# A recommender tower: one-hots move to GpSimd, selected fields change slots, loads and orders change

## The reference

```python
e = jnp.stack([tbl_0[ids[:, 0]], ..., tbl_49[ids[:, 49]]], axis=1)   # 512 x 50 x 16
gram = jnp.einsum('bid,bjd->bij', e, e)
z = gram[:, I, J]                                    # i < j, 1225 values
h = jnp.concatenate([z, dense_ctx], axis=1)
h = jnp.maximum(h @ W_top1 + b_top1, 0.0)            # 1241 -> 512
h = jnp.maximum(h @ W_top2 + b_top2, 0.0)            # 512 -> 256
y = h @ W_top3                                       # 256 -> 1
```

## Time and profile before

| | us |
|---|---|
| median of three runs (lowest, highest) | 158.98 (158.74, 159.48) |
| the profiled execution, its own time | 159.45 |
| its span, first to last instruction | 157.3 |
| PE busy | 127.8 (81%) |
| POOL busy | 124.7 (79%) |
| DVE busy | 110.6 (70%) |
| ACT busy | 44.4 (28%) |
| mean granted clock of PE | 0.975 |

### The profile page before, as it was taken

How to read it: one execution, slowest core, us unless ns; L and a number is a source line. 1 busy time by engine, 2 the same in 40 slices (tenths; PEclk the granted TensorE clock), 3 DMA queues, 4 the chain that set the end, 5 groups by cost and what they waited for, 6 DMA issues and landing times.

```text
span 157.3 us, 3325 instructions
## 1 busy us (share of the span) xinstructions
PE 127.8 (81%) x1323; PEld 111.9 (71%) x1323; DVE 110.6 (70%) x193; ACT 44.4 (28%) x77; POOL 124.7 (79%) x184
## 2 busy tenths in 40 slices
PE   0007875937698999999999989999995994999992
PEld 0007764827588679978959989886695983899991
DVE  1807899998899989998898894999953019344021
ACT  8930000232205220332071205204422018444020
POOL 2989898898998989899889889898988898982000
PEclk9999998696899999999999999999999999999998
DMA  3199999734380010000000100010000000000000
GB/s 84 35 358 419 442 417 317 279 116 119 125 256 15 6 6 4 10 7 4 10 6 4 10 4 6 11 10 6 4 10 6 4 10 4 10 6 6 0 0 1
DMA packets 6486, 12.40 MB, mean 79 GB/s; under 512 B 2077, under 2 KB 5414, under 8 KB 6342
## 3 DMA queue, kind: packets, MB, share of 16 engines
q1 hardware_dynamic: 3592, 11.46, 19.7%
q0 software_dynamic: 2880, 0.74, 5.6%
HBM read 12.17 MB, written 0.03 MB: 78 GB/s over the span
## 4 chain that ended last, share of the span: by engine, by line
POOL 70%; PE 14%; issue 9%; DMA 3%; ACT 2%; DVE 1%; DVEq 0%
POOL moving L294 50%; POOL spacer L300 20%; PE psm L818 4%; PE gram L811 4%; DMA moving<-tbl,ids_sb 2%; PE gram L818 2%; PE p L818 2%; DMA ids_sb<-in_ids 1%; PE gram L792 1%; PE pt L878 1%; ACT blocks L214 1%; DVE mcols L542 1%; ACT scols L344 0%; PE pt L868 0%; DVE h2w L604 0%
## 5 line engine op out<-in xcount | busy, mean ns | idle before, releaser
L294 POOL DMA_INDIRECT moving<-tbl,ids_sb x90 | 89.3, 992 | 17.4 <-issue 14.6
L777 PE MATMUL psm<-table,onehot 128*128 128x160 f32 x208 | 36.7, 326 | 19.3 <-DVE onehot L510 12.8
L777 PEld LDWEIGHTS psm<-table,onehot 128*128 128x128 f32 x208 | 32.2, 206 | 22.3 <-issue 12.8
L818 PE MATMUL p<-z,w_sb 128*128 128x128 f32 x312 | 39.3, 276 | 2.3 <-DVE z L225 2.3
L818 PEld LDWEIGHTS p<-z,w_sb 128*128 128x128 f32 x312 | 37.1, 192 | 3.6 <-ACT z L225 1.8
L300 POOL MEMSET spacer<- 128x288 f32 x90 | 35.4, 394 | 0.0
L498 DVE TENSOR_TENSOR picked<-psm,mask 128x480 f32<-128x480 f32 (+1 forms) x36 | 22.1, 634 | 4.5 <-PE psm L777 4.2
L214 ACT COPY blocks<-mcols 32x384 f32<-32x384 f32 (+3 forms) x20 | 15.4, 771 | 32.4 <-DVE mcols L542 21.2
L220 DVE COPY z<-gram 63x384 f32<-63x384 f32 (+1 forms) x20 | 9.6, 480 | 17.3 <-PE gram L811 14.0
L482 DVE TENSOR_REDUCE fixed<-picked 128x48 f32<-128x480 f32 (+1 forms) x36 | 21.3, 627 | 0.2
L767 PE MATMUL psm<-large_table,large_hot 125*128 125x400 f32 x48 | 16.9, 501 | 0.0
(11 more groups left out here) (50 smaller groups left out, 86.5 us busy)
## 6 DMA issues: line engine op xcount, KB each, us to landing
wide<-quotients SPq DMA_DIRECT2D x4, 896.0 KB, 8.2
w_sb<-in_w SPq DMA_DIRECT2D x1, 3072.0 KB, 17.4
large_table<-tbl SPq DMA_DIRECT2D x2, 781.2 KB
moving<-tbl,ids_sb POOLq DMA_INDIRECT x90, 2.8
table<-in_small SPq DMA_DIRECT2D x1, 720.0 KB, 7.2
table<-in_small SPq DMA_DIRECT2D x1, 640.0 KB, 8.7
w_sb<-in_w SPq DMA_DIRECT2D x1, 512.0 KB
table<-in_small SPq DMA_DIRECT2D x1, 480.0 KB, 5.9
```

Of the source, the lines that this page charges most:

```text
L294: nc.gpsimd.indirect_dma_start(moving[:, t, slot, 0:D], None, table, bass.IndirectOffsetOnAxis(ap=ids_sb[:, t, field:field + 1], axis=0),) ...
L777: ins = nc.tensor.matmul(psm[:, m % 2, (f - a) * R * D:(f - a + 1) * R * D], onehot[:, t % 2, f, :], table[:, f, :], start=True, stop=True)
L818: return nc.tensor.matmul(hidden_sums(t, k), w1_sb[:, c, P * k:P * (k + 1)], z[:, t % 2, c, :], start=first, stop=last)
```

## The change

- `SELECTED` becomes [1, 2, 2, 2]: one picked field of tile 0 is selected too (unit 9), so there are 89 gathers. The picked fields come first among the large ones and take the first two middle slots; `fold` writes there, and `turn_mid` waits for them, `turn_late` no longer.
- After gathers 13 to 21, 23 to 35 and 41 to 53, GpSimd makes one-hots of two small fields each (`pool_onehots`, 35 of them: fields 9 to 25 of tile 1, all of tiles 2 and 3) and no memset. VectorE no longer makes these; it was eight instructions of 8 or 9 fields.
- The two large tables are loaded ahead of w1. ids_t and consts are issued by ScalarE.
- The product of zeros goes: the first chunk starts the sum itself. So does the memset of `quot_t`. `large_masks` covers four tiles and has buffers of its own.
- The orders on ScalarE, VectorE and PE are written anew. On PE, product_y(0) now comes after ten selections of tile 0 and three of tile 1 (nine and five before).

The core of the diff:

```diff
-SELECTED = [0, 2, 2, 2]
+SELECTED = [1, 2, 2, 2]
-LARGE[len(LARGE) // 2 + 1:len(LARGE) // 2 + 1] = PICKED
+LARGE[0:0] = PICKED
+HOT_FIELDS = 2
+HOT_BEGINS = {1: 12, 2: 22, 3: 40}
+FIRST_HOT = {0: 26, 1: 9, 2: 0, 3: 0}
+VECTOR_HOTS = [3, 4, 4, 4]
...
         def _(sp):
             sp.dma_start(ids_sb[:], ids).then_inc(ids_loaded, 16)
-            sp.dma_start(ids_t_sb, ids_t).then_inc(ids_t_loaded, 16)
-            sp.dma_start(consts[:], consts_in).then_inc(consts_loaded, 16)
...
                 if t >= 2:
-                    sp.wait_ge(wide_ready, NWC * (t - 1))
+                    sp.wait_ge(wide_ready, VECTOR_HOTS[t - 2])
+                    if t > 2:
+                        sp.wait_ge(pool_ready, pool_hots(t - 2, NS))
                     sp.wait_ge(large_ready, sum(SELECTED[:t - 1]))
...
             load_wide(1)
+            for n in range(NP):
+                sp.dma_start(large_table[0:UNITS, n], tables[n].rearrange("(q p r) d -> p q (r d)", q=SPLIT, r=RL)
+                             ).then_inc(large_loaded, 16)
             sp.dma_start(w1_sb[:], w1.rearrange("p (c n) -> p c n", c=CH)).then_inc(w1_loaded, 16)
...
             load_wide(2)
-            for n in range(NP):
-                sp.dma_start(large_table[0:UNITS, n], tables[HALF + n].rearrange("(q p r) d -> p q (r d)", q=SPLIT, r=RL)
-                             ).then_inc(large_loaded, 16)
             load_wide(3)
...
+                count[0] += 1
+                for tile, began in HOT_BEGINS.items():
+                    first = FIRST_HOT[tile] + HOT_FIELDS * (count[0] - 1 - began)
+                    if FIRST_HOT[tile] <= first < NS:
+                        pool_onehots(tile, first, min(first + HOT_FIELDS, NS))
+                        return
+                clear_spacer()
+
+            def pool_onehots(t, a, b):
+
+                if a == FIRST_HOT[t]:
+                    pool.wait_ge(wide_loaded[t], 16)
+                    if t == 1:
+                        pool.wait_ge(consts_loaded, 16)
+                    else:
+                        pool.wait_ge(rows_made, unit(t - 2, NSC))
+                nc.gpsimd.tensor_scalar(onehot[:, t % 2, a:b, :],
+                                        wide[:, t % 2, P * a:P * b].rearrange("p (f b) -> p f b", b=P),
+                                        consts[:, 0:1], None, ALU.is_equal).then_inc(pool_ready, 1)
...
         def _(act):
+            act.dma_start(ids_t_sb, ids_t).then_inc(ids_t_loaded, 16)
+            act.dma_start(consts[:], consts_in).then_inc(consts_loaded, 16)
...
-                dve.wait_ge(mid_gathered[t], 16 * HALF)
+                dve.wait_ge(mid_gathered[t], 16 * (HALF - SELECTED[t]))
+                if SELECTED[t]:
+                    dve.wait_ge(folded, unit(t, NSC + SELECTED[t]))
...
-                    if n == 0 and whole == CH:
-                        nc.tensor.matmul(p1[:], quot_t[SIDE:SIDE + 1, 0:P], quot_t[SIDE:SIDE + 1, :],
-                                         start=True, stop=False)
                     for k in range(H1 // P):
-                        ins = chunk_sum(t, c, k, n == 0 and whole < CH, n == CH - 1 and k == H1 // P - 1)
+                        ins = chunk_sum(t, c, k, n == 0 and (k == 0 or whole < CH), n == CH - 1 and k == H1 // P - 1)
```

The new order up to product_y(0) and behind it, on VectorE (left: what stands between the last folds of tile 0 and the first unloading) and on PE:

```diff
             large_masks()
+            turn_smalls(0)
+            pick(0, 9)
+            onehots_large(1, 0)
+            fold(0, 9)
+            onehots_large(1, 1)
+            turn_mid(0)
             pick(1, 0)
+            copy_mid(0)
             pick(1, 1)
-            turn_smalls(0)
-            turn_mid(0)
             pick(1, 2)
-            copy_mid(0)
...
-            selections(0, 0, 9)
-            selections(1, 0, 5)
+            selections(0, 0, 10)
+            selections(1, 0, 3)
             product_y(0)
+            selections(1, 3, 5)
             layer0 = first_layer(0)
+            chunks(layer0, 1)
+            selections(1, 5, 7)
             chunks(layer0, 4)
...
+            chunks(layer0, 1)
+            product_y(1)
             second_layer(0)
-            product_y(1)
...
+            selections(2, 6, 9)
             product_x(1, 0)
+            selections(2, 9, 11)
+            chunks(layer1, 2)
...
+            chunks(layer1, 2)
+            selections(3, 4, 6)
+            product_y(2)
...
+            chunks(layer2, 2)
+            second_layer(1)
             product_x(2, 0)
-            chunks(layer2, 7)
+            chunks(layer2, 8)
             second_layer(2)
             product_y(3)
             second_bias(3)
+            layer3 = first_layer(3)
+            chunks(layer3, 2)
             product_x(3, 0)
-            layer3 = first_layer(3)
             chunks(layer3, 4)
             product_x(3, 1)
-            chunks(layer3, 5)
+            chunks(layer3, 4)
             product_x(3, 2)
-            chunks(layer3, 2)
+            chunks(layer3, 1)
             second_layer(3)
```

More of the change, by code:

```diff
@@ L71, with pool_hots @@
 CONSTS = 5 + SPLIT + RL
+HOT_BEGINS = {1: 12, 2: 22, 3: 40}
+FIRST_HOT = {0: 26, 1: 9, 2: 0, 3: 0}
+VECTOR_HOTS = [3, 4, 4, 4]
+def pool_hots(t, b):
+    return sum(-(-(NS - FIRST_HOT[n]) // HOT_FIELDS) for n in range(1, t)) + -(-(b - FIRST_HOT[t]) // HOT_FIELDS) if t else 0
 def unit(t, u):
@@ L492, in pick @@
                     a, b = u - NSC, u - NSC + 1
-                    rows, which = RL, large_mask[:, t - 1, a:b, :]
+                    rows, which = RL, large_mask[:, t, a:b, :]
                 k = b - a
@@ L609, in _ @@
             onehots(0, 2)
+            onehots_large(0, 0)
             pick(0, 0)
@@ L642, in _ @@
             unload_y(0)
-            onehots(1, 2)
-            onehots(2, 0)
-            onehots(2, 1)
-            onehots(2, 2)
             pick(1, 3)
             pick(1, 4)
+            fold(1, 3)
             turn_late(0, 0)
             pick(1, 5)
+            pick(1, 6)
             copy_late(0, 0)
-            fold(1, 3)
             fold(1, 4)
             fold(1, 5)
-            pick(1, 6)
+            fold(1, 6)
             pick(1, 7)
+            pick(1, 8)
+            fold(1, 7)
+            fold(1, 8)
             unload_x(0, 0)
-            pick(1, 8)
             unload_pairs(0)
-            fold(1, 6)
-            fold(1, 7)
-            pick(1, 9)
-            fold(1, 8)
-            fold(1, 9)
+            turn_smalls(1)
             onehots_large(2, 0)
+            smalls(1, 9, 10)
             onehots_large(2, 1)
-            turn_smalls(1)
-            pick(1, 10)
+            smalls(1, 10, 11)
+            turn_mid(1)
+            copy_mid(1)
             pick(2, 0)
-            fold(1, 10)
+            pick(2, 1)
             fold(2, 0)
-            pick(2, 1)
-            turn_mid(1)
+            fold(2, 1)
             pick(2, 2)
-            onehots(3, 0)
-            copy_mid(1)
-            fold(2, 1)
+            pick(2, 3)
             fold(2, 2)
-            onehots(3, 1)
-            onehots(3, 2)
-            pick(2, 3)
-            pick(2, 4)
             fold(2, 3)
             unload_y(1)
-            pick(2, 5)
-            fold(2, 4)
-            fold(2, 5)
+            last_layer(0)
+            smalls(2, 4, 6)
+            turn_late(1, 0)
+            copy_late(1, 0)
             pick(2, 6)
@@ L691, in _ @@
             fold(2, 7)
-            pick(2, 8)
-            last_layer(0)
-            fold(2, 8)
-            turn_late(1, 0)
+            smalls(2, 8, 9)
+            unload_x(1, 0)
+            unload_pairs(1)
+            turn_smalls(2)
             pick(2, 9)
-            copy_late(1, 0)
             pick(2, 10)
-            turn_smalls(2)
-            pick(3, 0)
             fold(2, 9)
             fold(2, 10)
-            unload_x(1, 0)
-            fold(3, 0)
-            unload_pairs(1)
-            pick(3, 1)
-            pick(3, 2)
-            fold(3, 1)
-            fold(3, 2)
             onehots_large(3, 0)
             onehots_large(3, 1)
+            pick(3, 0)
+            pick(3, 1)
+            fold(3, 0)
+            fold(3, 1)
             turn_mid(2)
+            copy_mid(2)
+            pick(3, 2)
             pick(3, 3)
-            copy_mid(2)
+            fold(3, 2)
             fold(3, 3)
@@ L719, in _ @@
             fold(3, 5)
-            last_layer(1)
-            smalls(3, 6, 7)
+            unload_y(2)
+            pick(3, 6)
             pick(3, 7)
-            pick(3, 8)
+            fold(3, 6)
             fold(3, 7)
-            fold(3, 8)
-            unload_y(2)
+            smalls(3, 8, 9)
+            pick(3, 9)
             turn_smalls(3)
             turn_late(2, 0)
-            pick(3, 9)
+            pick(3, 10)
             copy_late(2, 0)
             fold(3, 9)
-            smalls(3, 10, 11)
+            fold(3, 10)
+            last_layer(1)
             unload_x(2, 0)
@@ L988 @@
         "ids": ids.reshape(P, TILES * F),
```

(2 more changed lines are left out.)

104 lines of the change are left out of this document (47 added, 57 removed).

## The result

The changed kernel takes 185.59 us (median of 4 runs, 184.62 to 186.10) against 159.23 for the kernel before: ratio 1.165, 95% interval 1.158 to 1.171. The prediction said 161.0 with a range from 155.3 to 166.5. The direction was the forecast one, the size was far outside. The profiled execution took 185.38, its span is 182.3, 25.0 more than before. Some executions of a kernel take over 1.5% longer than its fastest, and the ratios leave those out.

A forecast was written before the change was run, and what follows sets the result against it. Gathers decide when the tail starts, PE its length. POOL: -1.47 - 2.5 + 3.2 + 5.0 = +4.2, less 2.2 slack, +2.0; PE +1.5; the later counts: span 159.3, median 161.0, range 155.3 to 166.5.

The forecast's parts named there:

- (c): On POOL, 35 one-hots of 256 elements replace memsets, at 0.45 us each: +3.2 us (bounds -0.9 and +6.9).
- 1.8 cycles an element: Second estimate for a POOL one-hot of 256 elements: 0.48 us in all, making the POOL sum 1 us higher.
- 2.2 us of slack: Between the last gather's columns being ready (145.48) and product_x(3,2) starting (147.66); taken off POOL's +4.2, leaving +2.0.
- the one-hots on POOL cost much: Rival, chance 0.12: at 0.55 us a one-hot the last gather moves 3.5 us more, median 164.5; at 0.65, 168.
- (d): On POOL, tile 2's first one-hot waits for wide(2) behind gather 23, from 39.3 to 45.1: +5.0 us (bounds 1 and 6).
- (b): Eight one-hots leave VectorE, so POOL's gathers and memsets are held up less: -2.5 us (bounds -4 and 0).
- (a): On POOL, one gather less: -1.47 us for the last gather.
- The large tables ahead of w1: Tables land at 32.3, so pick(0,9) starts at 35.1, not 31.0, and product_y(0) at 41.1, 4.6 us later.
- the half clock: PE's four 400-column products before pick(0,9) take 5.5 us at half clock; 2.8 was taken, 5.5 kept for the range.
- in time: Rival, chance 0.36: tables land by 28.2, product_y(0) starts at 37.0, PE ends 2.6 us earlier; span 154.7, median 156.4.
- PE after product_y(0): PE's stretch: 117.7 less 6.4 idling, plus 0.7 work and 2.6 remaining idling; last product at 155.7, +1.5 us.
- One-hots of GpSimd held up by VectorE's large ones: VectorE's two-input large one-hots may block POOL's one-hots, which read: at most 7 x 0.69 = 4.8 us.

The follow-up runs named there:

- form runs: Kernel before with its 90 memsets replaced by ten forms of instruction on scratch tiles, nine in a row each; TENSOR_SCALAR of 256 took 0.877 to 0.956 us, copies 0.40.
- d_dummy: Kernel before with 35 of its 90 memsets replaced by one-hots of a scratch tile that nobody reads; 191.44 us against 159.31, once.
- a_vector: Changed kernel with all one-hots back on VectorE and a memset behind every gather, large tables still early; 168.81 us against 159.31, ratio 1.064.
- h3_split: Changed kernel with one-hots back on VectorE and each large table loaded in two parts, 112 and 13 partitions; 158.95 us, ratio 1.004 (kernel before 158.62).
- h2_split: Same kernel as h3_split, run on a chip where the kernel before takes 184.94; 195.36 us, ratio 1.055.

## Why the prediction was wrong

*The step that failed* is (c) of POOL, the term "I take 0.45, between them since nothing is nearer to one: +0.09 x 35 = +3.2 (bounds -0.9 and +6.9)". It measured +24.9 (0.72 x 34 + 0.40). The price was drawn from the memset's rate, once for a write, twice for a read and a write. The form runs show that this is right for a copy (0.40, between 0.33 and 0.55) and wrong for TENSOR_SCALAR, which takes 2.6 ns an element. The upper bound of +6.9 was none: nothing in the trace of before said that the rate of one instruction of GpSimd holds for another. The estimate by the Trainium skill's 1.8 cycles an element ("GPSIMD Engine Reference", section 3.1) was too low for this instruction as well, 0.48 against 0.95; measured, 2.6 ns an element is some 3 cycles of the 1.2 GHz that the page gives, and the fixed part is three times the 0.10 that I put beside it. Section 4.1 of the same page of the Trainium skill has it that one-input work "is roughly line-rate"; the copies come nearer to that (0.40 us for 256 elements), this instruction doesn't.

*The mechanism around it was right in the main*: the gather queue decides when the tail starts, and a longer instruction there moves every later gather. d_dummy shows it with nothing else of the change. *The path was not*: the sum led from the last gather, less 2.2 us of slack, to product_x(3,2). The end hung at the last middle gather instead, where the kernel before has no slack either (product_y(3) waits 2.02 for it). By the prediction's path 25.4 less 2.2 would be 23.2 us; the measured 25.0 are 21.6 at product_y(3) and 3.4 in the tail. The rival "the one-hots on POOL cost much" had the mechanism, too, with 0.12 and a price of 0.55 to 0.65.

*(d), the stall at wide(2)*: forecast 5.0, measured 3.9; it began at 45.3, since the one-hots of tile 1 had already moved gather 23 by 6.6, and it ended at 49.2, not 45.1. So that the length came out near is partly luck. *(b), fewer hold-ups*: forecast -2.5, found -1.9 as the rest of a sum. *(a)* needs no measurement: it is one repeat of the queue less.

*The large tables ahead of w1*: forecast landing 32.3, measured 36.9; the half clock, which I put into the range only, came true, after PE had stood 12.7 us. 4.6 + 2.5 = 7.1 explain the 6.8 us by which product_y(0) was later than forecast. The rival "in time" falls. That the few engines are the cause, the split loads show. Why the landing was 4.6 later than the rate from the earlier trace rows isn't settled; w1 flowed beside the tables from 24 us on, which my sum left out.

*PE after product_y(0)*: the sum 117.7 - 6.4 + 0.7 + 2.6 = 114.6 was hidden in the change, but a_vector and h3_split lay it open: 114.8 us from product_y(0) to PE's last product in the first (47.54 to 162.29), 114.5 in the second (38.40 to 152.89). The total is so close partly by luck: PE idles 4.3 and 3.5 us, not 2.6, and is busy 110.5 and 111.0, not 112.0. Against the kernel before, h3_split gains 5.0 us from product_y(0) to product_y(3) (91.1 in place of 96.2) and loses 1.9 ahead of it and 1.7 in the tail; that is the 1.5 between the spans 155.8 and 157.3. The median of h3_split's ten runs, 158.95, is above what its profiled execution (157.57) gives: such a difference is beyond what a sum over one execution can tell.

*One-hots of GpSimd held up by VectorE's large ones*, by the Trainium skill's "SBUF — State Buffer", section on who interferes with whom: at most 4.8 us was put beside the sum. The trace of the changed kernel has two places where such instructions overlap, by 0.3 us each, and neither side takes longer than elsewhere. The first:

```profile
67.12 0.96 POOL L332 TENSOR_SCALAR onehot<-wide,consts 128x256 f32<-128x256 bf16 x1
67.75 0.69 DVE L559 TENSOR_TENSOR large_hot<-wide,consts 128x512 f32<-128x512 bf16 x1 [0.35 <-PE psm L796]
```

All 34 one-hots together take 0.6 us more than 34 x 0.95, so whatever held them up, it wasn't 4.8. Two short overlaps are too few to speak against the rule.

## What to carry to other kernels

An instruction that takes the place of another on the engine whose queue paces the kernel is priced by itself, in its own form, on the chip, before anything is arranged around it: ten forms fit in one run. A rate taken from another instruction of the same engine bounds nothing from above. A load that few DMA engines carry (125 partitions: 5.2 of 16 here) belongs behind everything that is urgent, or is cut so that most of it goes over more of them (112 + 13 for 125 brought it 10 us forward). And the slack of a queue is read at the first place where the limiting engine waits for it, here product_y(3), not at its last instruction.

## What the runs showed of the hardware that was not expected

TENSOR_SCALAR on GpSimd costs over twice a copy of the same size (0.95 and 0.40 us for 256 elements), in all types and both operations tried, and the gather behind it takes 1.03 us in place of 0.95.

Gathers that follow each other without a memset between them (every 1.25 us) leave VectorE waiting up to 14.5 us at a time for what the profile calls remote, and PE up to 15.4 us; the last such wait of VectorE ends at 126.8, 10 us after the last gather. The memsets may be there for that. It was one run, on a chip where the kernel before takes 200.7, and the cause wasn't isolated.

The same kernel before takes 158.6 to 159.3 in three groups of runs (the result's and two more) and 184.9, 186.7 and 200.7 in the other three. In the profiles of the latter (but for the run without memsets, where it is a pick that waits) VectorE waits, ahead of unloading a product, for something the profile calls remote; in h2_split PE has by its rows finished the product 4 to 5 us before the unloading starts (in all, how often, the longest):

```profile
DVE z L237 <- remote: 35.5, 5, 8.2
```

No such wait stands in any profile from a chip where the kernel before takes 159. In h2_split the last wait before an unloading ends at 139.11 and the last gather starts at 139.89, so the pauses seem to go with the gathers. A version's gain on one chip thus says little about another; why chips differ in it stays open.
